# Output projection in three float16 products, relative logits copied by ScalarE, statistics spread over 60 units, mask work moved into the attention

## The chip, the core and the metric

The kernel runs on one core of one Trainium2 chip. The metric is the device time of one execution in microseconds, the median of several. The core's engines are TensorE (PE, with its weight loads as PEld), VectorE (DVE), ScalarE (ACT), GpSimd (POOL) and SyncE (SP), which here only issues the DMAs. Each engine works through its own list in order; they meet at semaphores.

## The reference, cut to what matters

Halo attention over 8x8 windows with a 12x12 neighbourhood, its result added to x, a group norm, a mask over 32x32 tiles and a 3x3 convolution:

```python
qkv = einsum('bchw,oc->bohw', gn(x), W_qkv)          # x: (2, 128, 256, 256)
q, k, v = windows of 8x8 (q), windows of 12x12 with padding 2 (k, v), 4 heads of 32
attn = softmax(q * SCALE @ k.T + rel_pos_emb(q, rel_height, rel_width) + FIXED_MASK)
x1 = x + einsum('bchw,oc->bohw', attn @ v, W_out)     # the output projection
y = gn(x1)
out = conv3x3(y * tile_mask(y)) + bias                # a tile counts if max|y| > 1e-6
```

gn is a group norm over 32 groups of 4 channels and the whole image, one for each of the two batches. FIXED_MASK leaves each query only the keys of its own row and column parity, so the attention splits in 4 parities (PAR).

## The kernel before

There are three stages. In the first the weights are scaled and split in float16 halves, and the statistics of batch 0 of x are gathered (16 loads of 2 MB, `bn_stats` on DVE).

The second stage, the attention, walks over 128 units (UNITS; half a strip of 8 rows by 128 columns each, batch 0 first), and each unit over 4 groups (GROUPS). The order is written out by hand: each engine runs `body(u, ...)` for u from -3 to 131, and in it the loop over g with n = 4u + g. One pass of this loop is called a group below, and there are 512 of them (GT). In group n the engines work on different ages of data:

- PE: scores of n into ps_s (L470, float32, 16 products of 64 columns), first half of the transposes of n - 3 (L450), projections q and k of a piece of a later unit (L432, L437: three float16 products each), v of n - 3 (L484), the product with v of n - 4 into ps_o (L501), second half of the transposes, and the output projection of unit u - 2 into ps_y (L511: one float32 product of 256 columns).
- DVE: sums of the relative logits (L547, brel), softmax sums (L551), the copy of the relative logits from ps_s to rel (L556), reciprocal (L562), the addition of ps_y to x1 (L571), the addition of scores and relative logits (L580), row maxima (L586), statistics of the finished x1 (L592, g = 0), the spread of q (L600), tile maxima and minima of x1 (L607, g = 1 and 2), and in units 6 to 37 one `bn_stats` a group over batch 1 of x (L531; 8 rows are loaded a unit, into st).
- ACT: copies out of PSUM (L638, L656 transposes; L627 k; L645 v; L650 of, the attention output), the exponential (L660), the normalised x (L684, L692) and its float16 half (L702).
- POOL: outer sum erel (L719), division by the sum (L726), product with the shift mask (L735, two, out of rel), subtraction of the maxima (L742), the low float16 half of z (L749).

At unit 38 (GN) the moments of batch 1 of x are finished inside the attention: DVE aggregates, PE sums over groups (L428) and holds back its next projection until DVE is through, ACT takes a square root.

Between the second and the third stage all engines meet. `groupnorm_moments("gn1", (0, 1))` finishes the moments of x1 for both batches, then DVE makes the table of the mask: maxima over tiles (L783), a maximum over all partitions on POOL (L819, PARTITION_ALL_REDUCE), and the tables ctab and dtab of scale and shift of each tile and strip (L800 to L812). Then the third stage starts: two zero rows are written to x1 in DRAM, SP loads x1, ACT normalises (L911), POOL adds rows (L984), ACT and DVE split the result (L919, L966), PE multiplies (L892; 4608 float16 products of 512 columns), DVE adds into oc (L956).

## Time and profile before

| | |
|---|---|
| median of 3 runs | 3703.85 us (3702.18 to 3705.59) |
| the profiled execution | 3702.19 us, its span 3700.4 us |
| first scores (L470) to last scores | 123.0 to 2621.5 us |
| first product of the convolution | 2695.22 us |
| busy: PE, DVE, ACT, POOL | 94%, 91%, 80%, 70% |
| 16 DMA engines, mean | 38.4% |

How to read it: the span is the profiled execution's own, from first to last instruction; 1.8 us more lie around it in its time. Busy shares are means over stages with different limits, and PE's busy time counts overlapping products, so the stages have to be read one by one, by the distance from one start to the next.

### The profile page before, as it was taken

The numbers are of one execution on the slowest core, as the hardware profiler recorded it, in microseconds if no ns is written. First come the engines' busy times: TensorE is split into PE (matmuls) and PEld (weight loads), VectorE is DVE, ScalarE is ACT, GpSimd is POOL, SyncE is SP. The second block draws the span as 40 slices with busy tenths as digits, with TensorE's granted clock in tenths as the row PEclk, the third lists the DMA queues.
The fourth block names the chain that finished last, engine by engine and source line by source line (L and its number), as shares of the span: only waits on it lengthen the run. The fifth ranks groups of instructions, "written<-read, shape, count | busy, mean of one in ns | idle before, by whom it ended". The sixth has DMA issues, their size and how long they took to land. (4 is left out here: it accounts for less than half of the span.)

```text
span 3700.4 us, 127356 instructions
## 1 busy us (share of the span) xinstructions
PE 3491.4 (94%) x51718; PEld 2480.6 (67%) x51718; DVE 3349.1 (91%) x5626; ACT 2966.0 (80%) x5320; POOL 2575.1 (70%) x3344
## 2 busy tenths in 40 slices
PE   0799999998999999999999999999589999999999
PEld 0587777777888888888888888888434444444444
DVE  9699999999999999999999999999789888888887
ACT  0788888887999999999999999998377777777774
POOL 1677777776777777777777777777366666666664
PEclk9999999999999999999999999999799999999999
DMA  8244544443333333333333333333244434344332
GB/s 374 79 132 133 159 134 154 148 139 105 103 103 97 94 98 103 103 97 91 101 103 103 95 91 103 103 100 83 69 160 162 154 146 154 147 154 154 154 154 83
DMA packets 492549, 464.06 MB, mean 125 GB/s; under 512 B 9664, under 2 KB 469312, under 8 KB 469440
## 3 DMA queue, kind: packets, MB, share of 16 engines
q1 hardware_dynamic: 491968, 455.92, 38.4%
q8 instruction: 412, 6.75, 0.8%
q14 instruction: 169, 1.38, 0.1%
HBM read 321.40 MB, written 134.48 MB: 123 GB/s over the span
## 5 line engine op out<-in xcount | busy, mean ns | idle before, releaser
L984 POOL TENSOR_TENSOR sb_tf<-sb_cf 128x1024 f32<-128x1024 f32 x256 | 609.4, 2382 | 392.2 <-DVE sb_tl L966 370.3
L450 PE MATMUL ps_t<-sb_ident,sb_d 128*108 128x128 f32 x4096 | 662.3, 284 | 6.2 <-ACT sb_pt L638 1.9
L600 DVE TENSOR_TENSOR sb_qb<-ps_q,sb_own_head 128x1024 f32<-128x1024 f32 x512 | 621.1, 1213 | 14.9 <-PE ps_q L432 14.9
L470 PEld LDWEIGHTS ps_s<-sb_kf,sb_qb 128*64 128x64 f32 x16384 | 519.1, 138 | 171.5 <-issue 162.9
L719 POOL TENSOR_TENSOR sb_erel<-sb_brel 128x288 f32<-128x288 f32 x512 | 351.5, 686 | 395.6 <-DVE sb_brel L547 394.7
L892 PE MATMUL ps_c<-sb_th,sb_wc_h 128*128 128x512 f16 x1536 | 584.3, 380 | 40.3 <-DVE sb_tl L966 40.2
L470 PE MATMUL ps_s<-sb_kf,sb_qb 128*64 128x54 f32 x16384 | 585.6, 224 | 2.4 <-DVE sb_scores L580 2.4
L892 PE MATMUL ps_c<-sb_th,sb_wc_l 128*128 128x512 f16 x1536 | 583.3, 380 | 0.0
L892 PE MATMUL ps_c<-sb_tl,sb_wc_h 128*128 128x512 f16 x1536 | 583.2, 380 | 0.0
L749 POOL TENSOR_TENSOR sb_zl<-sb_zf,sb_zh 128x396 f16<-128x396 f32 x512 | 481.1, 940 | 83.1 <-ACT sb_zh L702 83.1
L735 POOL TENSOR_TENSOR sb_prod<-sb_rel,sb_shift 128x192 f32<-128x192 f32 x1024 | 502.1, 511 | 0.0
L919 ACT CAST sb_th<-sb_tf 128x1024 f16<-128x1024 f32 x256 | 263.9, 1043 | 258.9 <-POOL sb_tf L984 258.9
L450 PEld LDWEIGHTS ps_t<-sb_ident,sb_d 128*108 128x108 f32 x4096 | 410.6, 131 | 87.8 <-ACT sb_pt L638 12.1
L726 POOL TENSOR_TENSOR sb_d<-sb_scores,sb_srcp 128x288 f32<-128x288 f32 x512 | 342.6, 669 | 160.3 <-DVE sb_srcp L562 160.3
L966 DVE TENSOR_TENSOR sb_tl<-sb_tf,sb_th 128x1024 f16<-128x1024 f32 x256 | 420.0, 1641 | 20.4 <-ACT sb_th L919 20.3
L956 DVE SCALAR_TENSOR_TENSOR sb_oc<-ps_c,sb_wscale,sb_oc 128x1024 f32<-128x1024 f32 x256 | 322.6, 1281 | 86.2 <-PE ps_c L892 86.1
L911 ACT ACTIVATE sb_cf<-sb_xc,sb_dtab,sb_ctab 128x32 f32<-128x32 f32 (+2 forms) x768 | 357.2, 551 | 26.4 <-DMA sb_xc<-x 26.4
L484 PE MATMUL ps_v<-sb_wq_h,sb_zh 128*108 128x128 f16 x2048 | 369.9, 219 | 0.0
L484 PE MATMUL ps_v<-sb_wq_l,sb_zh 128*108 128x128 f16 x2048 | 369.9, 219 | 0.0
L484 PE MATMUL ps_v<-sb_wq_h,sb_zl 128*108 128x128 f16 x2048 | 369.9, 219 | 0.0
L627 ACT COPY sb_kf<-ps_k 128x576 f32<-128x576 f32 x512 | 331.6, 648 | 43.0 <-PE ps_k L437 42.7
L656 ACT COPY sb_pt<-ps_t 108x512 f32<-108x512 f32 x512 | 302.1, 590 | 75.7 <-PE ps_t L450 71.7
(117 smaller groups left out, 8228.0 us busy)
## 6 DMA issues: line engine op xcount, KB each, us to landing
sb_xb<-rows SPq DMA_DIRECT2D x128, 780.0 KB, 6.5
sb_xc<-x SPq DMA_DIRECT2D x64, 1280.0 KB, 5.4
sb_x<-rows SPq DMA_DIRECT2D x128, 512.0 KB, 4.1
x<-sb_x SPq DMA_DIRECT2D x128, 512.0 KB, 3.3
out<-sb_oc SPq DMA_DIRECT2D x64, 1024.0 KB, 3.9
sb_abuf<-rows SPq DMA_DIRECT2D x16, 2048.0 KB, 11.7
sb_st<-rows SPq DMA_DIRECT2D x32, 1024.0 KB, 9.3
sb_raw<-wconv SPq DMA_DIRECT2D x1, 576.0 KB, 3.7
```

The source lines that it names most:

```text
L450: last = pe.transpose(ps_t[0:KV, wj * 128:(wj + 1) * 128], d[:, at:at + KV], ident[:])
L470: last = pe.matmul(s_at, qb[:, qc:qc + QB], kf[:, kc:kc + KR], start=True, stop=True)
L484: last = pe.matmul(ps_v[0:KV, p * C:(p + 1) * C], z_at(z, vslot, p, GW * WK * vg, [[1, KV]]), w[:, 2 * C:3 * C], start=(c == 0), stop=(c = ...
L600: dve.tensor_tensor(view(qb, 0, 128, vh * QBW + p * NW * QB, [[QB, NW], [QN, HEADS], [1, QN]]), view(ps_q, 0, 128, 0, [[QN, NW], [0, HEADS ...
L719: pool.tensor_tensor(view(erel, 0, 128, 0, [[KN, PAIRS], [KS, KS], [1, KS]]), view(brel, 0, 128, 0, [[KS, PAIRS], [0, KS], [1, KS]]), view ...
L726: pool.tensor_tensor(view(d, 0, 128, b0 * DB, [[DSLOT, PAIRS], [1, KN]]), view(sp_, 0, 128, b0 * NS, [[KN, PAIRS], [1, KN]]), view(srcp, 0 ...
L735: last = pool.tensor_tensor(view(prod, 0, 128, ax * PAIRS * KS * QS, [[KS * QS, PAIRS], [QS, KS], [1, QS]]), view(rel, 0, 128, b0 * PAIRS ...
L749: pool.tensor_tensor(z_at(zl, vslot, p, 0, [[1, PLANE]]), view(zf, 0, 128, (vslot % 2) * PAR * PLANE + p * PLANE, [[1, PLANE]]), z_at(zh, ...
L892: last = pe.matmul(m_at, wt[:, tap], t_at(z), start=(c == 0), stop=(c == 8))
L911: last = act.activation(view(cf, 0, 128, c0 + off, dims), view(xc, 0, 128, r + off, dims), ACT.Identity, bias=dtab[:, col], scale=ctab[:, ...
L966: dve.tensor_tensor(view(tl, 0, 128, at, [[CW, PAIRROWS], [1, W]]), view(tf, 0, 128, k * TF, [[W, PAIRROWS], [1, W]]), view(th, 0, 128, at ...
L984: pool.tensor_tensor(tf[:, k * TF:(k + 1) * TF], view(cf, 0, 128, c0 + ra * W, [[2 * W, PAIRROWS], [1, W]]), view(cf, 0, 128, c0 + rb * W, ...
```

## The change

The output projection takes float16: W_out is split in wo_h and wo_l, ACT copies ps_o as float16 oh, DVE subtracts oh from ps_o into ol, and PE sums three products (oh wo_h, oh wo_l, ol wo_h) where one float32 product stood. PE's next product into ps_o, and ps_y, wait for ol in place of of. The copy of the relative logits moves from DVE to ACT, behind the first copy of the transposes. The statistics of batch 1 of x are gathered over units 0 to 59: 4 rows a unit (8 in units 0 to 3), loaded early and read by DVE at g = 3. Their moments are finished at unit 60, those of x1 of batch 0 at unit 70, and the mask's tables of batch 0 at unit 71, with a PARTITION_ALL_REDUCE on POOL. Only batch 1's moments and tables are left for the start of the third stage, where they stand in front of the lists of DVE and POOL; ACT waits for them only at the first strip of batch 1. The zero rows are written in unit 4.

```diff
-        wo = sb("wo", C, F32)
+        wo_h, wo_l = sb("wo_h", C, F16), sb("wo_l", C, F16)
...
+        def tile_extremes(dve, link, b):
+
+            hs, n = STRIPS // B, TR // B
+            for t, dst, op in ((tmax, ext[0], ALU.max), (tmin, ext[1], ALU.min)):
+                for h in range(2):
+                    link(dve.tensor_reduce(view(dst, 0, 128, b * n * TC + 4 * h, [[TC, n], [1, 4]]),
+                                           view(t, 0, 128, b * n * 8 * SPT + 4 * h, [[8 * SPT, n], [1, 4], [8, SPT]]),
+                                           AX.X, op))
+                part = tiles_of(dst, b)
+                link(dve.tensor_scalar(part, part, mean_t[:, b * hs:b * hs + 1],
+                                       rstd_t[:, STRIPS + b * hs:STRIPS + b * hs + 1], ALU.subtract, ALU.mult))
+
+            link(dve.scalar_tensor_tensor(tiles_of(ext[0], b), tiles_of(ext[1], b), -1.0, tiles_of(ext[0], b),
+                                          ALU.mult, ALU.max))
+
+        def row_tables(dve, link, b, all_channels):
+
+            hs, n, S8 = STRIPS // B, TR // B, CSTRIPS * TC
+            lo, hi = b * S8 // B, (b + 1) * S8 // B
+            rstd = rstd_t[:, STRIPS + b * hs:STRIPS + b * hs + 1]
+            dve.wait_ge(all_channels, 1)
+            link(dve.tensor_scalar(tiles_of(tabs, b), tiles_of(tabs, b), THRESHOLD, rstd, ALU.is_gt, ALU.mult))
+            for q in range(SPT):
+                dve.tensor_copy(view(ctab, 0, 128, S8 + lo + q * TC, [[SPT * TC, n], [1, TC]]),
+                                view(tabs, 0, 128, b * n * TC, [[TC, n], [1, TC]]))
+            dve.memset(ctab[:, lo:lo + TC], 0.0)
+            dve.memset(ctab[:, 2 * S8 + hi - TC:2 * S8 + hi], 0.0)
+            link(dve.tensor_scalar(nmean[:, b:b + 1], mean_t[:, b * hs:b * hs + 1], -1.0, None, ALU.mult))
+            dve.tensor_copy(ctab[:, lo + TC:hi], ctab[:, S8 + lo:S8 + hi - TC])
+            link(dve.tensor_copy(ctab[:, 2 * S8 + lo:2 * S8 + hi - TC], ctab[:, S8 + lo + TC:S8 + hi]))
+            link(dve.tensor_scalar(view(dtab, 0, 128, lo, [[S8, 3], [1, hi - lo]]),
+                                   view(ctab, 0, 128, lo, [[S8, 3], [1, hi - lo]]), nmean[:, b:b + 1], None, ALU.mult))
...
+            def gathered(u):
+
+                if 0 <= u < DOUBLE:
+                    return (2 * u, 2 * u + 1)
+                return (u + DOUBLE,) if DOUBLE <= u < HALVES - DOUBLE else ()
+
+            MOMENTS = {HALVES - DOUBLE: 1, UNITS // B + 6: 0}
+            MASK = UNITS // B + 7
...
+                    for k in gathered(u):
+
+                        row = H + k * (WS // 2) + PAD
+                        if k >= 2:
+                            sp.wait_ge(sem["st_used"], 2 * (k - 1))
+                        sp.dma_start(st[:, k % 2 * HALF:(k % 2 + 1) * HALF],
+                                     x_in[:, row:row + WS // 2, :].rearrange("p a b -> p (a b)")
+                                     ).then_inc(st_loaded[k % 2], 16)
+                    if u == DOUBLE:
+
+                        sp.wait_ge(sem["zeroed"], 1)
+                        for row in (0, ROWS + 1):
+                            sp.dma_start(x1_dram[:, row:row + 1, :].rearrange("p a b -> p (a b)"), zrow[:]
...
-                            need(pe, sem["of_done"], m)
+                            need(pe, sem["ol_done"], m)
...
-                                pe.wait_ge(sem["of_done"], (u - 1) * GROUPS)
+                                pe.wait_ge(sem["ol_done"], (u - 1) * GROUPS)
                             need(pe, sem["x1_done"], n - 2 * GROUPS)
                             ob = slot % 2
-                            pe.matmul(ps_y[:, 0:QP], wo[:], of[:, ob * 1024 + g * QP:ob * 1024 + (g + 1) * QP],
-                                      start=True, stop=True).then_inc(sem["y_mm"], 1)
+                            for c, (o, w) in enumerate(((oh, wo_h), (oh, wo_l), (ol, wo_h))):
+                                last = pe.matmul(ps_y[:, 0:QP], w[:], o[:, ob * 1024 + g * QP:ob * 1024 + (g + 1) * QP],
+                                                 start=(c == 0), stop=(c == 2))
+                            last.then_inc(sem["y_mm"], 1)
...
-                        if on(n, GT):
-                            dve.wait_ge(sem["s_mm"], n + 1)
-                            need(dve, sem["prod_done"], n - 1)
-                            dve.tensor_copy(view(rel, 0, 128, b0 * PAIRS * 2 * RN, [[2 * RN, PAIRS], [1, 2 * RN]]),
-                                            view(ps_s[g % 2], 0, 128, KN, [[KR, PAIRS], [1, 2 * RN]])
-                                            ).then_inc(sem["rel_out"], 1)
...
+                        if on(n - 5, GT):
+
+                            v, vslot, vg = (u - 1, slot - 1, g - 1) if g else (u - 2, slot - 2, GROUPS - 1)
+                            dims = [[QP, PAR], [1, GW * QN]]
+                            dve.wait_ge(sem["oh_done"], n - 4)
+                            need(dve, sem["y_mm"], (v - 1) * PAR)
+                            dve.tensor_tensor(view(ol, 0, 128, (vslot % 2) * 1024 + vg * GW * QN, dims),
+                                              view(ps_o, 0, 128, 0, [[GW * QN, PAR], [1, GW * QN]]),
+                                              view(oh, 0, 128, (vslot % 2) * 1024 + vg * GW * QN, dims), ALU.subtract
+                                              ).then_inc(sem["ol_done"], 1)
...
-                        if stat is not None:
-                            if g != 1:
-                                stat_pieces(stat, h, (0, 4, 1, 2)[g], (1, 0, 1, 2)[g])
-                        if moments_due and g == 0:
-                            moments_sums(dve, link, (1,), sem["gn_agg_done"])
-                        if moments_due and g == 2:
-                            moments_tables(dve, link, (1,), sem["gn_sqrt_done"])
+                        if g == 3:
+                            for k in gathered(u):
+                                dve.wait_ge(st_loaded[k % 2], (k // 2 + 1) * 16)
+                                for c in range(2):
+                                    at = UNITS * 6 + (2 * k + c) * 6
+                                    dve.bn_stats(stats[:, at:at + 6],
+                                                 st[:, k % 2 * HALF + c * 512:k % 2 * HALF + (c + 1) * 512]
+                                                 ).then_inc(sem["st_used"], 1)
+                        if u in MOMENTS:
+                            b = MOMENTS[u]
+                            if g == 0:
+                                moments_sums(dve, link[b], (b,), gn_sem[b]["agg_done"])
+                            if g == 2:
+                                moments_tables(dve, link[b], (b,), gn_sem[b]["sqrt_done"], edges=(b == 1))
+                        if u == MASK and g == 0:
+                            tile_extremes(dve, link[0], 0)
+                            dve.tensor_copy(ext[1][:, 0:1], ext[0][:, 0:1]).then_inc(sem["tiles_done"], 1)
+                        if u == MASK and g == 2:
+                            row_tables(dve, link[0], 0, sem["all_tiles"])
...
+                        if on(n, GT):
+                            act.wait_ge(sem["s_mm"], n + 1)
+                            need(act, sem["prod_done"], n - 1)
+                            act.copy(view(rel, 0, 128, b0 * PAIRS * 2 * RN, [[2 * RN, PAIRS], [1, 2 * RN]]),
+                                            view(ps_s[g % 2], 0, 128, KN, [[KR, PAIRS], [1, 2 * RN]])
+                                            ).then_inc(sem["rel_out"], 1)
...
-                            act.copy(view(of, 0, 128, ((slot - 1) % 2) * 1024 + g * GW * QN,
+                            act.copy(view(oh, 0, 128, ((slot - 1) % 2) * 1024 + g * GW * QN,
                                           [[QP, PAR], [1, GW * QN]]),
                                      view(ps_o, 0, 128, 0, [[GW * QN, PAR], [1, GW * QN]])
-                                     ).then_inc(sem["of_done"], 1)
+                                     ).then_inc(sem["oh_done"], 1)
...
+                        if u == MASK and g == 0:
+                            pool.wait_ge(sem["tiles_done"], 1)
+                            pool.partition_all_reduce(tiles_of(tabs, 0), tiles_of(ext[0], 0), 128, RMAX
+                                                      ).then_inc(sem["all_tiles"], 1)
...
-        groupnorm_moments("gn1", (0, 1))
...
-                sp.wait_ge(sem["pads"], 1)
-
-                sp.dma_start(x1_dram[:, 0:1, :].rearrange("p a b -> p (a b)"), zrow[:]).then_inc(sem["edges"], 16)
-                sp.dma_start(x1_dram[:, ROWS + 1:ROWS + 2, :].rearrange("p a b -> p (a b)"), zrow[:]
-                             ).then_inc(sem["edges"], 16)
-                sp.wait_ge(sem["edges"], 32)
...
+                    if j + 2 == CSTRIPS // B:
+                        act.wait_ge(sem["step_done"], TABLE_STEPS)
...
-                dve.memset(zrow[:], 0.0)
+                link = linker(dve, sem["step_done"])
+                moments_sums(dve, link, (1,), sem["agg_done"])
                 for z in (th, tl):
-                    last = dve.memset(view(z, 0, 128, 0, [[CW, 2 * NM * PAIRROWS], [CW - 1, 2]]), 0.0)
-                last.then_inc(sem["pads"], 1)
+                    dve.memset(view(z, 0, 128, 0, [[CW, 2 * NM * PAIRROWS], [CW - 1, 2]]), 0.0)
+                moments_group(dve, link, (1,), ps_c, sem["sum_done"])
+                moments_tables(dve, link, (1,), sem["sqrt_done"], edges=False)
+                tile_extremes(dve, link, 1)
+                dve.tensor_copy(ext[1][:, 0:1], ext[0][:, 0:1]).then_inc(sem["tiles_done"], 1)
+                row_tables(dve, link, 1, sem["all_tiles"])
...
+                pool.wait_ge(sem["tiles_done"], 1)
+                pool.partition_all_reduce(tiles_of(tabs, 1), tiles_of(ext[0], 1), 128, RMAX
+                                          ).then_inc(sem["all_tiles"], 1)
```

On DVE, in a group of g = 3 and the next of g = 0 in the middle of the attention (ps_o is the attention output in PSUM, oh its float16 copy), before:

```order
L600 TENSOR_TENSOR sb_qb<-ps_q,sb_own_head 128x1024
L547 TENSOR_REDUCE sb_brel<-sb_prod 128x96
L551 TENSOR_REDUCE sb_ssum<-sb_scores 128x8
L556 COPY sb_rel<-ps_s 128x144
L562 RECIPROCAL sb_srcp<-sb_ssum 128x8
L571 SCALAR_TENSOR_TENSOR sb_x<-ps_y,sb_oscale,sb_x 128x4x64
L580 TENSOR_TENSOR sb_scores<-ps_s,sb_erel 128x288
```

and on DVE in the same place of the changed kernel:

```order
L662 TENSOR_TENSOR sb_qb<-ps_q,sb_own_head 128x1024
L604 TENSOR_REDUCE sb_brel<-sb_prod 128x96
L608 TENSOR_REDUCE sb_ssum<-sb_scores 128x8
L613 RECIPROCAL sb_srcp<-sb_ssum 128x8
L622 SCALAR_TENSOR_TENSOR sb_x<-ps_y,sb_oscale,sb_x 128x4x64
L635 TENSOR_TENSOR sb_ol<-ps_o,sb_oh 128x4x64
L642 TENSOR_TENSOR sb_scores<-ps_s,sb_erel 128x288
```

The copy of rel is gone, and the subtraction into ol stands between the addition to x1 and that of the scores.

On ACT, one group in the middle of the attention, from the exponential to the next, in the changed kernel (before, the row of sb_rel is missing and sb_of stands for sb_oh; nothing else differs):

```order
L740 ACTIVATE sb_scores<-sb_scores,sb_alpha 128x288
L774 ACTIVATE sb_zf<-sb_xb,sb_shift_t,sb_rstd_t 128x2x65x4
L784 CAST sb_zh<-sb_zf 128x396
L712 COPY sb_pt<-ps_t 108x512
L716 COPY sb_rel<-ps_s 128x144
L701 COPY sb_kf<-ps_k 128x16x36
L725 COPY sb_vf<-ps_v 108x512
L730 CAST sb_oh<-ps_o 128x4x64
L736 COPY sb_pt<-ps_t 108x512
```

The copy of rel has the first copy of the transposes, and all of ACT's work before it, ahead of it in the list.

On POOL at unit 71 of the changed kernel, where g goes from 0 to 1 (ISA is an instruction that the compiler puts in where POOL goes over to PARTITION_ALL_REDUCE, itself the second ISA row, and again where it goes back):

```order
L824 TENSOR_TENSOR sb_scores<-sb_scores,sb_smax 128x288
L831 TENSOR_TENSOR sb_zl<-sb_zf,sb_zh 128x396
L837 ISA
L837 ISA sb_tile_abs<-sb_tile_ext 128x64
L801 ISA
L801 TENSOR_TENSOR sb_erel<-sb_brel 128x288
```

Before, these three ISA rows did not stand in the attention: L831 was followed by L801. They stood, of the whole table, between the stages. In the changed kernel they stand there too, for batch 1, right ahead of the third stage's additions. The same pair of ISA rows stands in the first stage of both kernels, the second of them ahead of L303.

## Rows read from the trace of the kernel before

**Rows 1.** Busy time by stage: length, PE, PEld, DVE, ACT, POOL (count), PEclk, DMA share, GB/s

```profile
640.00:880.00 240.00, 230.30 (x4307) 184.80 (x4304) 229.69 (x467) 200.34 (x386) 177.57 (x279) 1.00 0.45 138
...
1400.00:1640.00 240.00, 240.00 (x4580) 196.85 (x4579) 223.28 (x447) 216.35 (x411) 189.67 (x299) 1.00 0.35 95
...
2800.00:3600.00 800.00, 800.00 (x3697) 361.14 (x3696) 695.58 (x515) 585.16 (x867) 486.10 (x206) 1.00 0.40 153
```

**Rows 2.** Timeline of PE, two late groups: start us, us, engine, line, operation

```profile
1503.83 0.60 PE L511 MATMUL ps_y<-sb_of,sb_wo 128*128 128x256 f32 x2
...
1504.35 1.14 PE L470 MATMUL ps_s<-sb_kf,sb_qb 128*64 128x54 f32 x32
...
1505.91 0.30 PE L432 MATMUL ps_q<-sb_zh,sb_wq_h 128*128 128x256 f16 x1
...
1506.32 0.33 PE L437 MATMUL ps_k<-sb_zh,sb_wq_h 128*128 128x396 f16 x1
...
1506.49 0.33 PE L437 MATMUL ps_k<-sb_zh,sb_wq_l 128*128 128x396 f16 x1
...
1509.18 1.14 PE L470 MATMUL ps_s<-sb_kf,sb_qb 128*64 128x54 f32 x32
```

**Rows 3.** Timeline of DVE, an early group

```profile
873.50 0.54 DVE L547 TENSOR_REDUCE sb_brel<-sb_prod 128x96 f32<-128x384 f32 x1
...
874.32 0.30 DVE L556 COPY sb_rel<-ps_s 128x144 f32<-128x144 f32 x1
874.53 0.20 DVE L562 RECIPROCAL sb_srcp<-sb_ssum 128x8 f32<-128x8 f32 x1
874.64 0.44 DVE L571 SCALAR_TENSOR_TENSOR sb_x<-ps_y,sb_oscale,sb_x 128x256 f32<-128x256 f32 x1
874.99 0.45 DVE L580 TENSOR_TENSOR sb_scores<-ps_s,sb_erel 128x288 f32<-128x288 f32 x1
...
878.10 0.68 DVE L531 BATCH_NORM_STATS2 sb_stats<-sb_st 128x6 f32<-128x512 f32 x1
878.70 0.54 DVE L547 TENSOR_REDUCE sb_brel<-sb_prod 128x96 f32<-128x384 f32 x1
```

**Rows 4.** All instructions of L531: duration min/median/max, first and last start

```profile
L531 DVE BATCH_NORM_STATS2 sb_stats<-sb_st x128: 674/684/697, 238.4 to 882.8; 128x6 f32<-128x512 f32 x128
```

**Rows 5.** Waits, 400 to 1000 us: total us, times, longest

```profile
DVE sb_stats L531 <- DMA sb_st<-rows: 13.6, 22, 1.6
```

**Rows 6.** ACT groups of instructions, 1400 to 2000 us: busy us, mean ns, idle before

```profile
L627 ACT COPY sb_kf<-ps_k 128x576 f32<-128x576 f32 x125 | 81.1, 649 | 10.0 <-PE ps_k L437 10.0
...
L650 ACT COPY sb_of<-ps_o 128x256 f32<-128x256 f32 x124 | 46.2, 373 | 1.7
```

**Rows 7.** Timeline of PE around the moments of batch 1 (unit 38)

```profile
885.43 0.60 PE L511 MATMUL ps_y<-sb_of,sb_wo 128*128 128x256 f32 x2
...
899.54 0.60 PE L511 MATMUL ps_y<-sb_of,sb_wo 128*128 128x256 f32 x2
```

**Rows 8.** Timeline of DVE between the second and the third stage

```profile
2646.73 7.28 DVE L118 BATCH_NORM_AGGREGATE sb_aggr<-sb_stats 128x2 f32<-128x768 f32 x2 [0.33 <-PEq L317]
...
2664.70 0.29 DVE L792 SCALAR_TENSOR_TENSOR sb_tile_ext<-sb_tile_ext 128x128 f32<-128x128 f32 x1
2667.60 0.23 DVE L794 TENSOR_SCALAR sb_tile_abs<-sb_tile_abs 128x128 f32<-128x128 f32 x1 [2.60 <-POOL sb_tile_abs L819]
```

**Rows 9.** Timeline of POOL and of PE at the start of the third stage

```profile
2689.44 25.81 POOL L984 TENSOR_TENSOR sb_tf<-sb_cf 128x1024 f32<-128x1024 f32 x9 [21.94 <-ACT sb_cf L911]
...
2695.22 0.61 PE L892 MATMUL ps_c<-sb_th,sb_wc_h 128*128 128x512 f16 x1 [40.18 <-DVE sb_tl L966]
```

**Rows 10.** Timeline of POOL in the first stage

```profile
14.30 0.50 POOL L302 COPY sb_gw<-sb_rawn 128x384 f32<-128x384 f32 x1
25.36 0.98 POOL L303 TENSOR_TENSOR sb_gw<-sb_rawn 128x384 f32<-128x384 f32 x1 [10.56 <-issue]
```

**Rows 11.** Busy time, 10 to 26 us, as rows 1

```profile
10.00:26.00 16.00, 0.00 (x0) 0.00 (x0) 15.81 (x30) 0.00 (x0) 3.38 (x4) 1.00 1.01 429
```

162 lines of the change are left out of this document (59 added, 103 removed).

## The prediction

> **What bounds the kernel now.** I read the busy times by stage first, then the timelines of the engines inside a stage, then the place where the stages meet. The convolution (from 2716 us on) has PE busy from end to end [rows 1] and nothing in it changes; I carry it over as it is. The attention has two regimes. In its later part PE is never idle while DVE, ACT and POOL are busy 223, 216 and 190 of 240 us [rows 1]: PE sets the pace, and one group takes 1509.18 - 1504.35 = 4.83 us from one set of scores to the next [rows 2]. In units 6 to 37, where DVE also takes the statistics of batch 1, it is PE that waits (230 of 240 us) and DVE that is full [rows 1]; there 128 groups run from 238.4 us to one group behind 882.8 us [rows 4], (882.8 - 238.4)/127 = 5.07 us each. This is DVE's own list: a group with one long reduction and no statistics takes 878.10 - 873.50 = 4.60 us, a `bn_stats` 878.70 - 878.10 = 0.60 us more [rows 3]. Three groups of a unit have such a long piece (1.13 us, or two `bn_stats` over x1 of 0.60), one has none, so DVE needs about 4.33 us a group alone, 4.93 us with one statistic; the rest is the wait for the load of st, 13.6 us over about 117 groups, 0.12 us each [rows 5]. 4.33 + 0.60 + 0.12 = 5.05 us. So the model by starts holds within 0.02 us, and I use it for the change.
>
> **The products of the output projection.** From the start of the float32 product to the next scores PE takes 1504.35 - 1503.83 = 0.52 us [rows 2]. A float16 product of 396 columns takes 1506.49 - 1506.32 = 0.17 us [rows 2], 0.11 us for 256 columns; four passes of that are 0.44 us, and 0.08 us is what PE waits before it goes over to the narrow scores. Three float16 products make 0.33 + 0.08 = 0.41 us: 0.11 us gained a group. The dearest neighbour is q, three float16 products of 256 columns read in short runs, which take 1506.32 - 1505.91 = 0.41 us [rows 2]; at that price the projection takes 0.49 us and 0.03 us is gained. oh and ol are read in one run like k, so I take 0.11 us: PE needs 4.72 us a group (4.80 at the other end).
>
> **DVE.** The copy of rel frees 874.53 - 874.32 = 0.21 us. The subtraction into ol reads 256 elements from PSUM and 256 from SBUF, as the addition to x1 does, which takes 874.99 - 874.64 = 0.35 us [rows 3]; I take 0.36, with 0.49 (the scores, 288 elements, with their successor's wait) as upper end. DVE then needs 4.33 + 0.15 = 4.48 us a group without statistics. Spread statistics are two `bn_stats` a unit, 0.30 us a group: 4.78 us in units 4 to 59. They stand at g = 3, the one group without a long piece, so all four groups are about alike, and their load is issued at the head of the unit, three groups ahead, which removes the 0.12 us wait. In units 0 to 3 DVE has four a unit but up to unit 2 nothing of x1 to do; I take the first 24 groups as unchanged.
>
> **ACT.** A copy costs 649 ns at 576 and 373 ns at 256 columns [rows 6], so 373 - 112 x 0.86 = 277 ns at 144. ACT is busy 216 of 240 us, 4.35 us a group [rows 1]; 4.63 us with the copy, below 4.72, and less in truth because neighbours overlap. What is queued behind the new wait on ACT (for scores that PE finished before the transposes that the copy ahead of it waits for) is the copy of k; nothing there comes later than 0.28 us. POOL's product with the shift mask now waits for ACT's list instead of DVE's; POOL is busy 190 of 240 us [rows 1], so about 1 us a group is free to absorb it.
>
> **Sum of the steady groups.** 128 groups from 5.07 to 4.78: 37 us. 88 groups (units 38 to 59) from 4.83 to 4.78: 4 us. 272 groups from 4.83 to 4.72: 30 us. Together 71 us gained. Moments of batch 1 move from unit 38 to 60 at the same price.
>
> **What is put into the attention.** The moments of x1 of batch 0 (unit 70) are a second event like that of unit 38, where PE's projections stand 899.54 - 885.43 = 14.1 us apart instead of 4.83 [rows 7]: 9.3 us. There DVE was behind to begin with and now it is not; I take 8 us (5 to 10). The mask at unit 71 costs DVE some small operations, 1 us beyond its slack, and takes POOL out: it goes over to the all-reduce and back, each with an ISA row. The one such return that stands in the open is that ahead of L303, which waits for no semaphore and yet starts 10.56 us after the copy before it [rows 10]. There the DMA engines were full (1.01) [rows 11], in the late attention they are at 0.35 [rows 1], so I take 8 us for each of the two, with 0 and 10.56 as ends. The all-reduce takes 2.6 us as DVE sees it [rows 8], some 2 us on POOL itself. POOL is then away for 8 + 2 + 8 = 18 us; 0.8 us of that it would have idled, and PE can go on for one group less what the scores' chain needs, about 2.5 us. That leaves 15 us, and 2 us for refilling the chain: 17 us. With DVE's 1 us the mask costs 18 us (4 to 24), the two events 26 us.
> The Trainium skill (GPSIMD Engine Reference, section 2.1 Instruction dispatch) puts the first call to freshly loaded kernel code at approximately 6 us. This rule speaks against the move, as the row does; by its figure the mask would cost 14 instead of 18 us, and the whole would come out 6 us lower than below. The trace's one open switch is longer than that, and no row shows one under light load.
>
> **Between the stages.** DVE's last attention work ends at 2646.4 (0.33 us before the aggregate) and the first product of the convolution starts at 2695.22: 48.8 us [rows 8, 9]. Most of it is in series: moments, tables, a barrier, zero rows, load, normalisation, additions. After the change loads and ACT's first strips (tables of batch 0 are ready) run beside DVE's chain for batch 1, but POOL stands in the way: all-reduce first, then the switch back, then the additions. The chain: of what DVE does from 2646.4 to the end of the last operation before the all-reduce, 2664.99, the aggregate (7.28 us) is halved, 3.6 us less, and the edge tables, a barrier and half of the reductions' elements go, an estimated 3.6 us for a dozen operations of 0.2 to 0.6 us; 18.6 - 7.2 = 11.4 us are left; all-reduce 2.6 us; switch 8 us; from POOL's first addition to PE's first product 2695.22 - 2689.44 = 5.8 us as before [rows 9]. 27.8 us instead of 48.8: 21 us gained (18 with 10.56, 27 or so with 0, where ACT's strips come last). DVE's own tables end inside the switch. Zero rows and the split of wo cost 1 us at most, beside other work.
>
> **Sum.** 71 + 21 - 26 = 66 us gained, from 3702.2 us of the profiled execution to 3636; its time lies 1.7 us below the median, so the median would be 3638 us.
>
> **Rivals.** (1) As summed: 3638 us. Chance 0.50, its own range 3620 to 3652. (2) The switch is nearly free: with 0 instead of 8 us the mask costs 4, the crossing gains 6 more, 3618 us. For it: the only row of it lies beside full DMA engines. Against it: nothing else explains 10.56 us in front of an instruction without a wait. Chance 0.18. (3) The float16 products behave like q's: 272 x 0.08 = 22 us less gain, 3660 us. Against it: the reads are contiguous. Chance 0.12. (4) Engines that are now all within 8% of PE disturb each other: ACT's copy of rel comes behind up to 1.3 us of normalisation, POOL's product, the subtraction and the exponential follow late, and the late groups stay at 4.83: 30 us less gain, 3668 us. For it: 4.63, 4.48 and 4.72 are close. Against it: the chain from one exponential over POOL to the next is over 1 us shorter than a group, since only one copy of 0.28 us was added to it. Chance 0.12. (5) Slower: ol becomes the release of ps_o. Before, PE's next product with v needed ACT's copy only; now it needs DVE's subtraction one group later, behind five other DVE operations. Where that puts the 0.36 us in series with PE instead of beside it, every group pays it: 511 x 0.36 = 184 us against 66 gained, 3822 us; it decides from 66/511 = 0.13 us a group on. Against it: in DVE's order the subtraction ends about 1.6 us after the group's first reduction (873.50 to 874.99, less 0.21, plus 0.36 [rows 3]), and PE asks for ps_o only behind scores, transposes and three projections. Chance 0.06. The remaining 0.02 is no measurable change by several of these together.
>
> **The numbers.** Within 0.2% of before (7 us, about what a measurement of this kernel can tell from none) I put 0.02, faster 0.92, slower 0.06. The range must leave out no more than 2 in 10: it reaches from case 2 to case 4 with 4 to 12 us for what else is unknown in each (the ends of the events), 3606 to 3672 us.
>
> **What would show it.** In the profile after: groups of 4.72 us from the middle of the attention on (scores to scores), 0.41 us from the first output product to the scores; 4.78 us in units 4 to 59, DVE without idle time; no wait on the load of st; a hole of about 20 us in POOL's work at unit 71 of 128, and about 28 us from the last attention work of DVE to the first product of the convolution. I am wrong if PE waits for ol in front of L501's product in most groups, if late groups stay near 4.83, or if POOL's hole is under 5 us.

## The result, and the profile after

The changed kernel takes 3797.93 us (median of 4 runs, 3791.26 to 3800.92) against 3703.78 us before: ratio 1.0252, 95% interval 1.0234 to 1.0269. It is slower; 3638 us were predicted. The profiled execution of the changed kernel has a span of 3797.9 us.

The first reading is the length of the units. I take the starts of DVE's sums L604 (L547 before), four to a unit, and add their distances, in us of the profiled execution:

| kernel | units 1-3 | 4-59 | 60 | 61-69 | 70 | 71 | 72-125 |
|---|---|---|---|---|---|---|---|
| before | 55.8 | 1121.9 | 19.3 | 173.8 | 19.3 | 19.3 | 1042.6 |
| changed | 60.6 | 1216.7 | 29.7 | 174.0 | 29.2 | 33.4 | 1024.7 |

The late units gain 18 us, the three events (units 60, 70 and 71) cost 34 (9 of it moved here from unit 38), and units 4 to 59, where some 50 us less were expected (41 of the sum and those 9), take 95 us more. Between the stages 23 us are gained. So the loss is in the early units. Busy time there and later, which answers to [rows 1] (start and end of the stretch, its length, PE, PEld, DVE, ACT, POOL, PEclk, DMA share, GB/s):

```profile
640.00:880.00 240.00, 217.81 (x4092) 180.57 (x4092) 212.47 (x418) 199.07 (x407) 167.70 (x264) 0.96 0.39 112
...
2000.00:2240.00 240.00, 238.24 (x4697) 199.10 (x4696) 228.34 (x452) 224.68 (x468) 191.74 (x303) 1.00 0.38 103
```

In the early stretch no engine is full. DVE, nearly full before and expected full now, idles 27.5 of 240 us. PE, which stands idle for 22 us, is granted a mean clock of 0.96 here, so for some 7% of the stretch the lower of its two levels, 1.2 instead of 2.4 GHz; before it was 1.00 [rows 1]. Who waits for whom there, 400 to 1000 us (who waits, for whom, then total us, times, longest):

```profile
POOL sb_erel L801 <- DVE sb_brel L604: 159.8, 111, 4.1
...
DVE sb_stats L677 <- DMA sb_st<-rows: 55.9, 28, 3.0
PE ps_o L565 <- DVE sb_ol L635: 53.6, 29, 3.2
ACT sb_oh L730 <- PE ps_o L565: 51.1, 30, 3.2
```

The last three look like one wait passed along, by their counts (28, 29, 30, one a unit in 28 units): DVE waits for st, then PE for DVE's ol, then ACT for PE. Where it begins is seen in the order of SP's transfers in one unit, and what DVE does meanwhile:

```profile
749.21 0.37 SPq L452 DMA_DIRECT2D x<-sb_x  x1
762.41 0.37 SPq L462 DMA_DIRECT2D sb_x<-rows  x1
762.82 0.58 SPq L470 DMA_DIRECT2D sb_st<-rows  x1
763.44 0.44 SPq L446 DMA_DIRECT2D sb_xb<-rows  x1
770.70 0.37 SPq L452 DMA_DIRECT2D x<-sb_x  x1
```

```profile
761.17 1.21 DVE L669 TENSOR_REDUCE sb_tmin<-sb_x 128x4 f32<-128x1024 f32 x1
762.29 0.54 DVE L604 TENSOR_REDUCE sb_brel<-sb_prod 128x96 f32<-128x384 f32 x1
...
764.88 1.21 DVE L662 TENSOR_TENSOR sb_qb<-ps_q,sb_own_head 128x1024 f32<-128x1024 f32 x1
767.98 1.29 DVE L677 BATCH_NORM_STATS2 sb_stats<-sb_st 128x6 f32<-128x512 f32 x2 [1.89 <-DMA sb_st<-rows]
```

SP issues the load of st 0.41 us behind the load of x1, and this waits until DVE's minimum at g = 2 has read x1 (it ends at 762.38). The load lands in about 5 us; DVE wants it 3.7 us after the minimum, at 766.09, and gets it at 767.98. Before the change the load of st (L397) stood ahead of the store (L403) and the load of x1 (L413) in SP's list:

```profile
753.55 0.37 SPq L413 DMA_DIRECT2D sb_x<-rows  x1
753.96 0.58 SPq L390 DMA_DIRECT2D sb_xb<-rows  x1
754.59 2.03 SPq L397 DMA_DIRECT2D sb_st<-rows  x1
760.30 0.37 SPq L403 DMA_DIRECT2D x<-sb_x  x1
```

It too was issued soon after a load of x1, but it opened the list of the next unit, and so was early for its reader. SP's own waits in the changed kernel, in the same 600 us, show how long it stands at the two:

```profile
SPq L462 <- DVE sb_tmin L669: 266.8, 27, 10.3
SPq L452 <- DVE sb_x L622: 188.7, 28, 7.3
```

The late groups do what [rows 2] led me to expect. PE, from the output products to the scores, and the next scores:

```profile
2005.67 0.27 PE L576 MATMUL ps_y<-sb_oh,sb_wo_h 128*128 128x256 f16 x1
2005.78 0.27 PE L576 MATMUL ps_y<-sb_oh,sb_wo_l 128*128 128x256 f16 x1
2005.89 0.27 PE L576 MATMUL ps_y<-sb_ol,sb_wo_h 128*128 128x256 f16 x1
2006.09 1.14 PE L534 MATMUL ps_s<-sb_kf,sb_qb 128*64 128x54 f32 x32
...
2010.82 0.39 PE L534 MATMUL ps_s<-sb_kf,sb_qb 128*64 128x54 f32 x6
```

0.42 us (0.41 predicted), and 4.73 us in this group (4.72). The mean over units 72 to 125 is 4.74 (1024.7/216). POOL around the mask of unit 71:

```profile
1654.96 0.94 POOL L831 TENSOR_TENSOR sb_zl<-sb_zf,sb_zh 128x396 f16<-128x396 f32 x1
1661.84 0.54 POOL L837 PARTITION_ALL_REDUCE sb_tile_abs<-sb_tile_ext  x1 [5.94 <-PE ps_t L514]
1669.27 0.68 POOL L801 TENSOR_TENSOR sb_erel<-sb_brel 128x288 f32<-128x288 f32 x1 [6.89 <-issue]
```

POOL is away 1669.27 - 1655.90 = 13.4 us where 18 were predicted: 5.94 and 6.89 us idle on the two sides of a reduction of 0.54 us. The Trainium skill (GPSIMD Engine Reference, section 2.1 Instruction dispatch) has approximately 6 us for a first call to freshly loaded code; by that rule, the trace agrees on the way out, and the way back costs as much again. Not all of the 5.94 us is loss: the reduction reads DVE's tile extremes, which are ready only at 1658.32 (the copy of L688 starts at 1658.17 and takes 0.15), so that POOL would have stood idle for 2.4 us of it in any case. Between the stages, what answers to [rows 8, 9]:

```profile
2766.71 3.62 DVE L118 BATCH_NORM_AGGREGATE sb_aggr<-sb_stats 128x2 f32<-128x768 f32 x1 [0.33 <-PEq L367]
...
2777.60 0.55 POOL L1002 PARTITION_ALL_REDUCE sb_tile_abs<-sb_tile_ext  x1 [28.60 <-DVE sb_tile_ext L967]
...
2786.51 7.93 POOL L1013 TENSOR_TENSOR sb_tf<-sb_cf 128x1024 f32<-128x1024 f32 x3 [8.37 <-issue]
...
2792.29 0.61 PE L909 MATMUL ps_c<-sb_th,sb_wc_h 128*128 128x512 f16 x1 [20.93 <-DVE sb_tl L992]
```

From the end of DVE's attention work, 2766.38, to the first product are 25.9 us (27.8 predicted, 48.8 before). POOL waited 28.6 us for DVE ahead of the reduction and then started it at 2777.60, so that its way out cost nothing here.

### The profile page after: what moved, and what is told of

Its sections match the earlier page's. It is cut to its first block and busy times, and to the rows that moved or that the text cites. A ratio compares the mean times of both kernels' runs of the same rounds, so it can differ in the third digit from the quotient of the medians.

```text
span 3797.9 us, 129440 instructions
## 1 busy us (share of the span) xinstructions
PE 3486.2 (92%) x52232; PEld 2513.6 (66%) x52232; DVE 3405.9 (90%) x5647; ACT 3042.4 (80%) x5835; POOL 2575.7 (68%) x3345
## 5 line engine op out<-in xcount | busy, mean ns | idle before, releaser
L514 PE MATMUL ps_t<-sb_ident,sb_d 128*108 128x128 f32 x4096 | 674.9, 288 | 3.5 <-ACT sb_pt L736 2.0
L801 POOL TENSOR_TENSOR sb_erel<-sb_brel 128x288 f32<-128x288 f32 x512 | 352.4, 688 | 455.1 <-DVE sb_brel L604 444.4
L534 PEld LDWEIGHTS ps_s<-sb_kf,sb_qb 128*64 128x64 f32 x16384 | 536.1, 141 | 121.4 <-issue 96.8
L534 PE MATMUL ps_s<-sb_kf,sb_qb 128*64 128x54 f32 x16384 | 603.4, 228 | 10.6 <-DVE sb_scores L642 10.6
L831 POOL TENSOR_TENSOR sb_zl<-sb_zf,sb_zh 128x396 f16<-128x396 f32 x512 | 483.8, 945 | 82.1 <-ACT sb_zh L784 82.1
L514 PEld LDWEIGHTS ps_t<-sb_ident,sb_d 128*108 128x108 f32 x4096 | 418.3, 133 | 83.6 <-issue 5.8
L565 PE MATMUL ps_o<-sb_pt,sb_vf 108*32 108x64 f32 x16384 | 338.6, 223 | 132.2 <-DVE sb_ol L635 123.6
L565 PEld LDWEIGHTS ps_o<-sb_pt,sb_vf 108*32 108x32 f32 x16384 | 260.0, 110 | 178.1 <-issue 147.8
```

The lines of the kernel that those rows point to most:

```text
L514: last = pe.transpose(ps_t[0:KV, wj * 128:(wj + 1) * 128], d[:, at:at + KV], ident[:])
L534: last = pe.matmul(s_at, qb[:, qc:qc + QB], kf[:, kc:kc + KR], start=True, stop=True)
L565: last = pe.matmul(o_at, v_at, p_at, start=True, stop=True)
L801: pool.tensor_tensor(view(erel, 0, 128, 0, [[KN, PAIRS], [KS, KS], [1, KS]]), view(brel, 0, 128, 0, [[KS, PAIRS], [0, KS], [1, KS]]), view ...
L831: pool.tensor_tensor(z_at(zl, vslot, p, 0, [[1, PLANE]]), view(zf, 0, 128, (vslot % 2) * PAR * PLANE + p * PLANE, [[1, PLANE]]), z_at(zh, ...
```

## The experiments

The edits are shown cut to what matters; "..." and the words behind # stand for code that is left out. The time of a run is the median, with the lowest and the highest in brackets; lengths of units are from its profiled execution. "The first" is the first experiment.

Theory: the load of st is late because of its place in SP's list, and all the loss is that. Rivals: ol as release of ps_o stands in series with PE (case 5 of the prediction; the wait for ol is the largest of PE in the profile's page, 123.6 us); or the many small loads are themselves slow or in the way.

**SP's order.**

```
 def body(u, s, slot, on):            # SP
     ... load of xb
+    for k in gathered(u): ... load of st
     ... store of x1
     ... load of x1
-    for k in gathered(u): ... load of st
```

> The changed kernel with one edit: SP issues the load of st at the head of a unit, right behind the load of xb, ahead of the store and the load of x1. My theory (the load of st comes late because it is queued behind the load of x1, which waits for DVE's minimum of x1 at g = 2 of the same unit): DVE's wait for the load of st at g = 3 (55.9 us in the 600 us from 400 on) falls to under 2 us, PE's wait for ol falls with it, units 4 to 59 go from about 21.9 to about 19.5 us (DVE's own list, 4.87 us a group), the time is 3797.9 - 57 x 2.3 = 3667 us (3650 to 3680). Rival A (ol as release of ps_o stands in series with PE): the wait for ol stays, 3780 to 3800 us. Rival B (64 small loads in 60 units are slow or disturb the other transfers, wherever they stand): DVE's wait stays, 3780 to 3800 us.

Measured: 3671.87 us (3671.67 to 3672.59), ratio to before 0.9914 (0.9897 to 0.9930). 126 us of the changed kernel's time go with this edit. The wait for st is gone from the list of waits, that of PE for ol is

```profile
PE ps_o L565 <- DVE sb_ol L635: 0.7, 2, 0.4
```

(53.6 us before the edit, with the same ol). Units 4 to 59 take 1094.6 us, 4.89 us a group. Both rivals fall. PE's granted clock from 640 to 880 us is 1.00 again, so the lower clock followed from the wait; what part of the 126 us came by way of it the runs do not separate. SP's timeline shows what the place really does: the load is still issued soon after the load of x1,

```profile
760.84 0.37 SPq L470 DMA_DIRECT2D sb_x<-rows  x1
761.26 0.73 SPq L446 DMA_DIRECT2D sb_xb<-rows  x1
762.04 1.65 SPq L454 DMA_DIRECT2D sb_st<-rows  x1
```

but it is now the one for the next unit: at the head of its list for unit u, SP stands at the time of unit u - 1, g = 2.

**The same loads, read one unit later.**

```
-for k in gathered(u):                # DVE, g == 3
+for k in gathered(u - 1) + (gathered(u) if u == HALVES - DOUBLE - 1 else ()):
```

> The changed kernel with SP's order as it is, but DVE reads the halves loaded in unit u at g = 3 of unit u + 1 (those of unit 59 still in 59), so that the same loads, issued at the same places, have four groups more to land. My theory (only the lateness against its reader counts): the same as with the load issued first, 3667 us (3650 to 3680), with one late read left in unit 59. Rival A (ol in series): 3780 to 3800 us. Rival B (the transfers themselves disturb others, such as the store and load of x1 or xb): SP's order is the same, so most of the loss stays, over 3750 us.

Measured: 3674.75 us (3673.14 to 3680.59). SP's order is that of the changed kernel, and the loss is gone all the same. What counts is the distance between the issue and its reader.

**The load between the store and the load of x1.**

```
 ... load of xb                       # SP
 ... store of x1
+for k in gathered(u): ... load of st
 ... load of x1
-for k in gathered(u): ... load of st
```

> The changed kernel with one edit: the load of st stands between the store and the load of x1, so that it is still behind the wait of the store (for the last addition to x1) and no longer behind that of the load of x1 (for DVE's minimum). My theory (only the wait for the minimum, three groups into the unit, comes too late; the store's wait ends in the unit's first group and the load lands in 5 us): as with the load at the head, 3672 us (3668 to 3678). Rival (the store's wait is late too): 3690 us or more.

Measured: 3673.40 us (3671.42 to 3674.11). Of the two waits ahead of the load only that for the minimum does harm.

**Without ol** (on top of the first edit; the third product reads oh in place of ol, so this kernel leaves the low part of the attention output out of its result).

```
-dve.tensor_tensor(ol, ps_o, oh, ALU.subtract).then_inc(ol_done)
-need(pe, sem["ol_done"], m)
+need(pe, sem["oh_done"], m)
-for c, (o, w) in enumerate(((oh, wo_h), (oh, wo_l), (ol, wo_h))):
+for c, (o, w) in enumerate(((oh, wo_h), (oh, wo_l), (oh, wo_h))):
```

> As the first (load of st at the head of the unit), and without the subtraction into ol: the third product of the output projection reads oh once more, so PE's work is the same and the low part of the attention output is left out; ps_o is released by ACT's copy as before the change. My theory: DVE has 0.33 us less a group, units 4 to 59 become bound by PE at 4.72 instead of about 4.87 us (0.15 x 228 = 34 us less than the first), late groups stay at 4.72: 3633 us (3620 to 3645). If ol is in series with PE anywhere in the late groups, these fall too, below 4.72, and the time is under 3610 us. If DVE's load does not matter in units 4 to 59, the time is that of the first within 5 us.

Measured: 3618.50 us (3616.88 to 3619.28), 53 us less than the first, where I expected 34 (the time is below the range that I gave). Units 4 to 59 take 1056.4 us (38 less), 4.72 a group: PE is full there (busy 240.00 of 240 us from 640 on), as expected. The other 15 us come from other places, also late: units 1 to 3, 61 to 69 and the events together 9, units 72 to 125 6. That DVE decides there for a while is argued, not shown. The usual late group does not change (the median is 4.72 us with and without ol), so ol is not in series with PE.

**With the float32 output projection** (on top of the first edit).

```
-for c, (o, w) in enumerate(((oh, wo_h), (oh, wo_l), (ol, wo_h))):
-    last = pe.matmul(ps_y, w, o, start=(c == 0), stop=(c == 2))
+pe.matmul(ps_y, wo, of, start=True, stop=True)     # of by ACT, float32; no ol
```

> As the first (load of st at the head of the unit), but the output projection as before the change: one float32 product, ACT copies to of, no ol. My theory: late groups are 4.83 instead of 4.72 us (272 x 0.11 = 30 us more), in units 4 to 59 PE binds at 4.83 instead of DVE at 4.87 (9 us less): 3688 us (3675 to 3700), so the three float16 products are worth some 20 us in all. If the projection's price were something else than PE's rows say, for example because DVE's subtraction costs more than the products gain, this kernel is as fast as the first or faster.

Measured: 3671.38 us (3670.10 to 3671.53). Here I was wrong: I expected 16 us more than the first was measured to take, and there is no difference. By units: 72 to 125 take 17.0 us more; units 4 to 59 take 14.3 less, units 1 to 3 2.5 less, the three events 0.8 less, 61 to 69 0.6 less. The three float16 products gain late, on PE, what their subtraction costs early, on DVE.

**With the copy of rel back on DVE** (on top of the first edit).

```
-act.copy(rel, ps_s[g % 2]).then_inc(rel_out)
 dve.tensor_reduce(ssum, ...)
+dve.tensor_copy(rel, ps_s[g % 2]).then_inc(rel_out)
 dve.reciprocal(srcp, ssum)
```

> The changed kernel with the load of st at the head of the unit (3671.9 us), and the copy of rel back on DVE, between the sum and the reciprocal, where it stood. My theory: in units 4 to 59 DVE is what binds (4.89 us a group), and the copy costs it what it did before less the wait for the sum that it hid, 0.36 + 0.21 - 0.48 = 0.09 us, 232 x 0.09 = 21 us more; in the late groups DVE's list grows to about 4.6 us, still under PE's 4.72, no change: 3693 us (3685 to 3700). Rival (the move to ACT is worth the 0.21 us that I put down for it in the prediction): 232 x 0.21 = 49 us more, 3720 us. Rival (ACT or POOL, not DVE, binds early): faster than 3671.9 us.

Measured: 3685.72 us (3685.33 to 3688.20), 14 us more than the first. Units 4 to 59 take 17.2 us more, 0.08 us a group. A copy that stood in the gap between the sum and the reciprocal, and was put down at 0.21 us, was worth 0.08. The gap is seen in DVE's list of the first experiment:

```profile
873.80 0.44 DVE L608 TENSOR_REDUCE sb_ssum<-sb_scores 128x8 f32<-128x288 f32 x1
874.28 0.20 DVE L613 RECIPROCAL sb_srcp<-sb_ssum 128x8 f32<-128x8 f32 x1
874.40 0.43 DVE L622 SCALAR_TENSOR_TENSOR sb_x<-ps_y,sb_oscale,sb_x 128x256 f32<-128x256 f32 x1
874.75 0.41 DVE L635 TENSOR_TENSOR sb_ol<-ps_o,sb_oh 128x256 f16<-128x256 f32 x1
875.08 0.45 DVE L642 TENSOR_TENSOR sb_scores<-ps_s,sb_erel 128x288 f32<-128x288 f32 x1
875.56 0.45 DVE L648 TENSOR_REDUCE sb_smax<-sb_scores 128x8 f32<-128x288 f32 x1
```

The reciprocal, which waits for the sum, starts 0.48 us after it, the maximum 0.48 after the addition.

**POOL without the switch in unit 71** (on top of the first edit; the maximum over the partitions is left out, so that the mask of batch 0 comes from each partition's own extremes).

```
-pool.partition_all_reduce(tiles_of(tabs, 0), tiles_of(ext[0], 0), 128, RMAX)
+pool.tensor_copy(tiles_of(tabs, 0), tiles_of(ext[0], 0))
```

> The changed kernel with the load of st at the head of the unit (3671.9 us), and in unit 71 POOL copies the tile extremes instead of reducing them over the partitions, so that POOL never leaves its usual code; the mask of batch 0 is then taken from each partition's own extremes. My theory: POOL's 13.4 us away (5.9 before the all-reduce, 6.9 behind it) is what unit 71 loses, it falls from 33.5 to about 20.5 us: 3659 us (3655 to 3663). Rival (DVE's own operations for the mask cost most of it): unit 71 stays above 26 us, 3665 us or more.

Measured: 3664.41 us (3660.79 to 3669.30), 7.5 less than the first and just above the range that I gave (3655 to 3663). Unit 71 takes 23.4 instead of 33.5 us (20.5 expected), so the switch costs 10.1 us, and what is left of the mask, DVE's small operations and whoever waits for them, 4.5 (against four groups of 4.72), where I had put 1. POOL is one that waits for them:

```profile
1534.96 0.24 POOL L837 COPY sb_tile_abs<-sb_tile_ext 128x64 f32<-128x64 f32 x1 [2.46 <-DVE sb_tile_ext L688]
```

Without these 2.5 us and the copy's own 0.24, the 13.4 us of POOL's absence come to 10.7, close to the 10.1 that were lost. The whole gained less than unit 71, since units 72 to 125 were 3.7 us slower in this profiled execution than in the first's.

**DVE's order** (on top of the first edit).

```
 dve.tensor_reduce(ssum, ...)
+dve.scalar_tensor_tensor(x1, ps_y, ...)
 dve.reciprocal(srcp, ssum)
-dve.scalar_tensor_tensor(x1, ps_y, ...)
-dve.tensor_tensor(ol, ps_o, oh, ...)
 dve.tensor_tensor(scores, ps_s, erel, ALU.add)
+dve.tensor_tensor(ol, ps_o, oh, ...)
 dve.tensor_reduce(smax, scores, ...)
```

> The changed kernel with the load of st at the head of the unit (3671.9 us), and DVE's order changed in two places: the addition to x1 stands between the sum and its reciprocal, the subtraction into ol between the addition to the scores and their maximum, so that neither the reciprocal nor the maximum waits for the operation just before it. Nothing is left out. My theory (units 4 to 59 are bound by DVE's list of 4.89 us, in which the reciprocal starts 0.48 instead of 0.36 us after the sum and the maximum 0.48 after the addition): 0.12 to 0.13 us saved twice, 4.64 us, PE's 4.72 binds: 232 x 0.17 = 39 us less, 3633 us (3628 to 3645). Rival (the later maximum delays POOL and ACT, or the subtraction, now later, holds up PE's next product with v): half of it or less, over 3650 us.

Measured: 3634.38 us (3632.75 to 3635.98), 37.5 less than the first (39 expected), with the same operations:

```profile
876.84 0.44 DVE L608 TENSOR_REDUCE sb_ssum<-sb_scores 128x8 f32<-128x288 f32 x1
877.20 0.47 DVE L618 SCALAR_TENSOR_TENSOR sb_x<-ps_y,sb_oscale,sb_x 128x256 f32<-128x256 f32 x1
877.59 0.19 DVE L625 RECIPROCAL sb_srcp<-sb_ssum 128x8 f32<-128x8 f32 x1
877.72 0.46 DVE L632 TENSOR_TENSOR sb_scores<-ps_s,sb_erel 128x288 f32<-128x288 f32 x1
878.09 0.41 DVE L641 TENSOR_TENSOR sb_ol<-ps_o,sb_oh 128x256 f16<-128x256 f32 x1
878.43 0.44 DVE L648 TENSOR_REDUCE sb_smax<-sb_scores 128x8 f32<-128x288 f32 x1
```

From sum to maximum are now 1.59 us, 1.76 before; no more, since PE binds again. Units 4 to 59 take 1059.7 us, 4.73 a group.

**The maximum over the partitions on PE and DVE, for both batches between the stages** (on top of DVE's order).

```
-pool.partition_all_reduce(tabs, ext[0], 128, RMAX)      # unit 71, and between the stages
+pe.transpose(ps_c[:, 512:640], ext[0], ident)
+dve.tensor_reduce(most, ps_c[:, 512:640], AX.X, ALU.max)
+dve.tensor_scalar(diag, ident, most, None, ALU.mult)
+pe.matmul(ps_c[:, 1024:1152], ones, diag, start=True, stop=True)
+for b in range(B): row_tables(dve, link, b, all_tiles, ps_c[:, 1024:1152])
```

> As the kernel with DVE's order changed, and the maximum over the partitions made by PE and DVE between the stages, for both batches at once (a transpose, a maximum, a diagonal, a product with ones), so that POOL never changes to the all-reduce. Nothing is left out. My theory: 13.4 us less in unit 71; between the stages the switch of 8.4 us goes, but ACT's first strips (6.7 us) now wait for the tables of batch 0, which come some 8 us later than before: about 1 us more. 3633 - 12 = 3621 us (3614 to 3628). Rival (the first strips are ready sooner than that, or POOL's start is not tied to the switch): below 3614 us.

Measured: 3623.81 us (3622.27 to 3626.89), ratio to before 0.9788 (0.9771 to 0.9804). Unit 71 falls from 35.6 to 20.8 us; from DVE's aggregate to the first product of the convolution 27.6 us pass instead of 25.5, as ACT's first strip comes later.

**The same with the float32 output projection**, by the edit shown above for it.

> As the kernel with DVE's order changed and the maximum over the partitions on PE and DVE (3623.8 us), but with the output projection as before the change: one float32 product, no ol. With the load of st moved alone this projection cost nothing (3671.4 against 3671.9 us), where I had expected 16 us. My theory for that: PE gained 0.11 us a group and DVE's list grew by the subtraction, and in units 4 to 59 and in the two events DVE was what bound. Where DVE's order takes its list below PE's, the float16 products must pay in full: 232 + 260 groups x 0.10 to 0.11 = 51 us, less some 5 us in the events: 3670 us (3660 to 3678). Rival (the products gain in the late groups only, for another reason): 3645 us or less.

Measured: 3660.18 us (3659.61 to 3661.17), 36 us more than with float16 products (46 expected, at the edge of my range). Units 4 to 59 cost 22.3 us more, 72 to 125 20.8, 0.10 us a group in both; units 1 to 3 take 2.3 less and the other units with them about the same. My count of 51 us had taken in all units alike. So the float16 products do pay, as soon as DVE has room for the subtraction.

**The maximum of batch 0 made in units 128 to 130** (on top of the maximum on PE and DVE).

```
+if u == UNITS: pe.transpose(ps_q, ext[0][:, 0:64], ident)
+if u == UNITS + 1 and g == 2: ... dve: most, diag of batch 0
+if u == UNITS + 1: pe.matmul(ps_k, ones, diag, ...)     # behind the unit's last group
+if u == UNITS + 2 and g == 1: row_tables(dve, link[0], 0, all_tiles, ps_k)
```

> As the kernel with the maximum over the partitions on PE and DVE (3623.8 us), but for batch 0 it is made in units 128 to 130, where PE has only output projections left, so that ACT's first strips need not wait for it between the stages. Nothing is left out. My theory: between the stages the strips (6.7 us) start behind ACT's root, about 9 us earlier, and POOL, which waits for them and for no switch, too; in the last units DVE has 2.3 us more to do: 3617 us (3613 to 3621). Rival (DVE's chain for batch 1 ends last between the stages): within 3 us of 3623.8 us.

Measured: 3625.42 us (3624.63 to 3629.60), no gain. ACT's first strip starts 5.8 us after DVE's aggregate instead of 15.0, POOL's first addition 12.5 instead of 21.8, but the aggregate itself is 4.7 us later (2.7 of it for the work in units 128 to 130), and then DVE's copies for the tables of batch 1 take 8.68 us beside POOL's first four additions:

```profile
2605.62 8.68 DVE L202 COPY sb_ctab<-sb_tile_abs 128x64 f32<-128x64 f32 x4
```

```profile
2604.99 9.26 POOL L1029 TENSOR_TENSOR sb_tf<-sb_cf 128x1024 f32<-128x1024 f32 x4 [32.64 <-ACT sb_cf L947]
```

**The tables of batch 1 spread later, in strip 2** (on top of that).

```
-row_tables(dve, link, 1, all_tiles, ps_c[:, 1024:1152])
+row_tables(dve, link, 1, all_tiles, ps_c[:, 1024:1152], rest=False)   # the flags alone
+if j == 2: row_tables(dve, link, 1, None, None, flags=False)           # in the strips' loop
```

> As the kernel with batch 0's maximum made in units 128 to 130 (3625.4 us), but of the tables of batch 1 only the flags, which DVE reads from PSUM, are made between the stages; the copies and products that spread them over the rows come in strip 2 of the convolution, long before strip 32 needs them. Nothing is left out. There the four copies of 64 elements on DVE took 8.68 us in place of 0.50 while POOL made its four first additions (2604.99 to 2614.25), and DVE's first low part came only at 2615.73. My theory (DVE's copies out of SBUF and POOL's additions keep each other out, one operation of DVE for each of POOL's): the low parts follow ACT's casts at once, the first product comes some 7 us earlier, 3618 us (3615 to 3622). Rival (the copies were slow for another reason, or DVE and POOL lose the same time in strip 2): within 2 us of 3625.4 us.

Measured: 3623.40 us (3616.78 to 3625.71), 2 us less than the one it builds on, within what separates runs: the rival's figure, not mine. The mechanism showed, most of the gain did not. The copies no longer stand there, and from DVE's aggregate to the first product 18.3 us pass (24.5 without the edit, 27.6 with the maximum between the stages). Of these 6.2 us some are lost again: the convolution took 1007.1 us from its first product to the end, 1005.8 in the other. In strip 2, where the tables are now made, one of the four copies again takes 2.35 us beside an addition of POOL (the other three 0.18), a low part comes late, and PE stands idle:

```profile
2664.23 0.39 PE L929 MATMUL ps_c<-sb_th,sb_wc_h 128*128 128x512 f16 x1 [1.63 <-DVE sb_tl L1017]
```

From the aggregate to the end of the kernel 5.0 us are gained in the profiled execution; but its aggregate comes 3.1 us later than in the other (units 1 to 3, 1.6 of it), though the two kernels have the same code up to there. These 3 us are a difference between two single executions, and they are as large as what is left of the gain, so the runs do not show whether the edit pays.

## Why the prediction was wrong

**The step that failed**: "their load is issued at the head of the unit, three groups ahead, which removes the 0.12 us wait". The diff puts it at the end of SP's list for the unit, behind the load of x1 and its wait for DVE's minimum at g = 2 ("loaded early", as the section on the change says, is the same mistake). The wait did not go, it grew to some 2 us a unit for DVE. Three edits, two of the issue's place and one of the reader's, do nothing but lengthen the distance between the two, and each brings back 123 to 126 us. I had listed the queues past which steps are moved, but not SP's.

With that one wait out of the way the kernel stands at 3671.9 us, 34 above the prediction. By terms:

- **PE, 4.72 us**: right (the median late group is 4.72); worth 0.10 to 0.11 us a group wherever DVE has room. q's price for the products (case 3) did not come.
- **DVE, 4.78 us in units 4 to 59**: it is 4.89, 25 us in all. The copy of rel was priced at its distance to the next operation, 0.21 us, but it filled the wait of the reciprocal for the sum; without it 0.08 are gained. The subtraction takes 0.33 from its start to the next (0.36 predicted).
- **The first units**, "I take the first 24 groups as unchanged": 3 us more up to unit 1 and 3 in units 1 to 3, where four `bn_stats` stand in one group. Without the subtraction the second 3 are gone (55.8 us, as before the change).
- **Moments of batch 0, 8 us**: 9.9 (29.2 instead of 19.3). **Mask, 18 us**: 14.1 (33.4 instead of 19.3); POOL's part was too large (two switches of 8 us, measured 5.9 and 6.9, and 2.4 of the 5.9 POOL would have waited anyway), DVE's too small (1 us, measured 4.5 with those who wait for it). The 14 us that the prediction works out with the 6 us that the Trainium skill has (GPSIMD Engine Reference, section 2.1 Instruction dispatch) meets the measured 14.1 in part by luck, since the 1 us for DVE stands in it too.
- **Between the stages, 21 us gained**: 22.9.
- **ACT**: the copy takes 0.28 us as predicted; POOL waits for it late in the attention, PE does not, so case 4 did not come.
- **The late units**, 272 groups at 0.11 us: in the first experiment units 61 to 69 and from 72 on gained 20 us of some 28. Three of the groups from unit 72 on are 1.3 to 1.4 us longer than the rest in the changed kernel. In them PE stands still in the middle of its product with v and waits for nothing that the profile shows, not for ol:

```profile
1990.67 0.43 PE L565 MATMUL ps_o<-sb_pt,sb_vf 108*32 108x64 f32 x15 [1.16 <-issue]
```

Such groups are missing before the change and in all three kernels without the subtraction; with DVE's order changed they are rare and shorter. Their cause is open.

- **Rival 5** had the right side and nearly the right time (3822 us) for a reason that the runs refute: PE does wait for ol, but because DVE is late, and the wait is gone with DVE's lateness while ol stays. That its side came true is luck. "I am wrong if PE waits for ol" was the right thing to look for, and the count told the causes apart: PE waits in one group of four, the one with `bn_stats`, and not in most.

The sum for the first experiment from these: 3638 + 25 (DVE) + 6 (first units) + 2 (moments) - 4 (mask) - 2 (crossing) + 8 (the late units) = 3673 us, measured 3671.9. The terms are rounded and read from the same traces, so the sum shows only that nothing large is missing.

## What to carry to other kernels

When a transfer is moved or re-cut, write down the whole list of the queue that issues it and the waits ahead of it: it is issued when the slowest of them ends, whatever its own condition, and the reader's slack is counted from there. A wait that shows at several engines with the same count, once a unit, may be one wait passed along; look for the first, and take it away to see whether the others go. An operation that stands between a producer and its dependent successor on one engine is worth less than its duration, and placing independent work in such gaps gained 37 us here at no cost, more than the whole change with its load put right (32 us); it also decided whether the cheaper products of PE were worth anything.

## What the hardware showed that I had not expected

DVE's copies of 64 elements from SBUF take 0.50 us for four when POOL is idle, and 8.68 us, 1.77 to 2.39 each, beside POOL's additions of 2.3 us (9.26 for four): one gets through for each of POOL's. In strip 2 of the last experiment one of four took 2.35 us beside an addition. A `tensor_scalar` of the same size that read from PSUM at 2605.30, also beside POOL's addition, took 0.28 us, as in the kernel where POOL was idle. The Trainium skill (SBUF — State Buffer, section "SBUF: two separate sides") says that DVE in a two-port mode, or with two inputs in SBUF, and POOL hold a shared pair of ports exclusively for a whole instruction, and that a float32 copy within SBUF runs in such a mode; by that rule, the trace agrees, down to the length of the delay.

POOL's change to the all-reduce and back took 5.9 and 6.9 us within the attention and 8.4 back between the stages, for 0.54 us of work. A transpose, a maximum, a diagonal and a product with ones on PE and DVE did the same in 2.2 us without a switch (from the last tile extreme at 2598.31 to the flags at 2600.53, in the kernel with the maximum on PE and DVE).
